# Graph-convolution passes: the load of a block's keys moved ahead of a store, and an index copy moved ahead of ScalarE's one-hots

## The reference

```python
def gcn_conv(x, w, b, row, col, ew, n):
    h = x @ w
    deg = jax.ops.segment_sum(ew, col, num_segments=n)
    dinv = jnp.where(deg > 0, jax.lax.rsqrt(deg), 0.0)
    norm = dinv[row] * ew * dinv[col]
    out = jax.ops.segment_sum(norm[:, None] * h[row], col, num_segments=n)
    return out + b
```

## Time and profile before

| | |
|---|---|
| median of 3 runs | 13451.6 us (13446.46 to 13469.0) |
| the profiled execution, its time | 13464.2 us |
| the profiled execution, its span | 13462.3 us |
| DVE busy over the span | 10894.3 us (81%) |
| PE busy over the span | 9747.7 us (72%) |
| POOL busy over the span | 8948.1 us (66%) |
| ACT busy over the span | 5666.9 us (42%) |

### The profile page before, as it was taken

One profiled execution on the slowest core, in us unless ns is written; L12 is line 12 of the kernel. 1 busy time (PEld: TensorE's weight loads), 2 busy tenths in 40 slices (PEclk: granted clock), 3 DMA queues, 4 the chain that ended last, 5 costly groups with the idle time before them and its releaser, 6 DMA issues. The chain is left out here.

```text
span 13462.3 us, 216102 instructions
## 1 busy us (share of the span) xinstructions
PE 9747.7 (72%) x59425; PEld 8272.6 (61%) x59425; DVE 10894.3 (81%) x23907; ACT 5666.9 (42%) x15747; POOL 8948.1 (66%) x9054
## 2 busy tenths in 40 slices
PE   5666667777756767766764556996997899678886
PEld 4555556666645555555553115886886899667775
DVE  8888878887858888888887996775776888689997
ACT  3444434444423333333333333664564455223332
POOL 6777757776667777777776004666666777677776
PEclk8888879999968888888886666998998999789997
DMA  3333323433323333333334772221221222133332
GB/s 90 89 86 88 89 71 119 124 119 116 121 60 101 101 97 99 100 101 101 100 97 164 272 272 57 49 50 40 49 49 41 54 55 56 32 78 87 85 87 68
DMA packets 627763, 1250.19 MB, mean 93 GB/s; under 512 B 201329, under 2 KB 380982, under 8 KB 577122
## 3 DMA queue, kind: packets, MB, share of 16 engines
q1 hardware_dynamic: 322624, 922.04, 19.8%
q0 software_dynamic: 290752, 265.79, 11.1%
q10 hardware_dynamic: 14337, 61.82, 1.2%
HBM read 482.46 MB, written 768.08 MB: 93 GB/s over the span
## 5 line engine op out<-in xcount | busy, mean ns | idle before, releaser
L1049 PE MATMUL p_slots<-part,one_lo 128*128 128x208 f32 (+1 forms) x20384 | 2841.9, 302 | 360.1 <-ACT one_lo L1016 304.5
L1049 PEld LDWEIGHTS p_slots<-part,one_lo 128*128 128x128 f32 x20384 | 2779.2, 197 | 423.0 <-ACT one_lo L1016 330.2
L995 POOL DMA_INDIRECT rows<-gcn_table,index x2156 | 2132.2, 989 | 1104.5 <-issue 591.3
L1376 PE MATMUL a_p_slots<-att_part,a_one_lo 128*128 128x456 f32 x8232 | 2008.4, 409 | 587.0 <-DVE y L1439 504.4
L1376 PEld LDWEIGHTS a_p_slots<-att_part,a_one_lo 128*128 128x128 f32 x8232 | 1742.2, 214 | 957.1 <-DVE y L1439 684.4
L1307 POOL DMA_INDIRECT sent<-a_out_rows,a_place x1568 | 1584.0, 1010 | 494.9 <-issue 475.6
L623 PE MATMUL p_slots<-x_part,key_lo 128*128 128x448 f32 x6916 | 1676.5, 398 | 114.8 <-DVE scratch L752 78.4
L557 POOL DMA_INDIRECT msg<-x_rows,index x1372 | 1309.3, 954 | 509.1 <-issue 448.1
L557 POOL DMA_INDIRECT msg<-h_rows,index x1274 | 1230.6, 966 | 529.0 <-issue 384.9
L623 PEld LDWEIGHTS p_slots<-x_part,key_lo 128*128 128x128 f32 x6916 | 1399.9, 209 | 234.4 <-DVE scratch L752 95.5
L789 DVE SCALAR_TENSOR_TENSOR run<-run,keep,msg 128x129 f32<-128x129 f32 (+1 forms) x3136 | 1116.7, 356 | 399.9 <-ACT msg L592 295.4
(11 more groups left out here) (481 smaller groups left out, 18358.1 us busy)
## 6 DMA issues: line engine op xcount, KB each, us to landing
running_dst<-a_run SPq DMA_DIRECT2D x98, 1600.0 KB
running_src<-s_run SPq DMA_DIRECT2D x98, 1600.0 KB
running<-run SPq DMA_DIRECT2D x98, 1032.0 KB
running<-run SPq DMA_DIRECT2D x98, 1024.0 KB
running<-y SPq DMA_DIRECT2D x98, 656.0 KB
s_rows<-sent ACTq DMA_DIRECT2D x98, 584.0 KB, 6.9
begun_x<-zeros SPq DMA_DIRECT2D x98, 512.0 KB
a_xdst<-begun_x SPq DMA_DIRECT2D x98, 512.0 KB
```

The source lines that it names most:

```text
L995: pool.indirect_dma_start(out=rows[h][:, KS[h] + k, :], out_offset=None, in_=table, in_offset=offsets(index[h][:, k:k + 1])).then_inc(gath ...
L1049: ins = nc.tensor.matmul(to, one_lo[h][:, q, e:e + P], flat(part[:, q, :, :]), start=q == 0 and part_no == 0, stop=q == CLASSES - 1 and pa ...
L1376: ins = nc.tensor.matmul(to[:, k, 0:WIDE_COLUMNS], one_lo[h][:, q, e:e + P], part[:, q, :], start=q == 0 and part_no == 0, stop=q == WIDE_ ...
```

## The change

In SP's order, the load for block n + 1's parity (it brings the keys of block n + 3) now stands ahead of the store of block n; the first load and the last two stores stand outside the loop. In ACT's order, `stage_index` stands ahead of `light`. Nothing else changes: the same instructions with the same waits are there.

```diff
@@ graph_pass, sync engine @@
-            with sp.Fori(0, IT) as i:
+            def renew(h, n):
+
+                sp.wait_ge(stepped, INIT + per * (n - 1) + ONE_HOTS)
+                sp.sem_inc(sig["rounds"].sem, 1)
+                sp.wait_ge(lit.sem, lit.base + n + 1)
+                load(h, n + 2)
+
+            def store(h, n):
+
+                sp.wait_ge(copied, n + 3)
+                sp.dma_start(running_v[:, bass.ds(n * B, B), :], run_rows[h][:]).then_inc(stored[h], 16)
+
+            renew(0, 0)
+            with sp.Fori(0, IT - 1) as i:
                 for h in range(2):
                     n = 2 * i + h
-
-                    sp.wait_ge(stepped, INIT + per * (n - 1) + ONE_HOTS)
-                    sp.sem_inc(sig["rounds"].sem, 1)
-                    sp.wait_ge(lit.sem, lit.base + n + 1)
-                    load(h, n + 2)
-
-                    sp.wait_ge(copied, n + 3)
-                    sp.dma_start(running_v[:, bass.ds(n * B, B), :], run_rows[h][:]).then_inc(stored[h], 16)
+                    renew(1 - h, n + 1)
+                    store(h, n)
+            renew(1, 2 * IT - 1)
+            for h in range(2):
+                store(h, 2 * IT - 2 + h)
@@ graph_pass, scalar engine @@
+                    act.wait_ge(gathered[h], 16 * GATHERED[h] * (i + 1))
+                    stage_index(h, (n + 2) * B)
+
                     act.wait_ge(looked, 2 * n + 4)
                     light(h, n + 2, i + 2)
-
-                    act.wait_ge(gathered[h], 16 * GATHERED[h] * (i + 1))
-                    stage_index(h, (n + 2) * B)
```

## The result

The changed kernel takes 13133.2 us (median of 4 runs, 13117.58 to 13146.72) against 13455.94 for the kernel before (4 runs): a ratio of 0.9759, 95% interval 0.9742 to 0.9776. The forecast was 13164 with a range down to 13138. The direction and the mechanism were right; the gain is 323 us in place of 288, and the time lies 5 us beyond the range's fast end.

The account below looks back on a forecast made before the run. A circle of waits through ACT's keys was taken to bound passes 1 and 2, POOL to bound pass 3. Savings of 129 + 147 + 14 - 2 = 288 us gave 13164 us, range 13138 to 13240.

Parts of the forecast that it names:

- Everybody waits for ACT, and ACT waits for a DMA behind a store.: Passes 1 and 2: a circle of copy, store, load and light sets the pace; ACT waits 352.9 us for keys.
- ACT's wait for keys goes to nothing; the tightest reserve is DVE's one-hots with 0.75 us.: Passes 1 and 2: keys land 6 us early; one-hots are ready at 7.25 us, PE wants them at 8.0.
- The light's wait for gathers stays within its 2.8 us: Passes 1 and 2: light has 2.8 us to spare; gathers landing later than that after PE's end would delay PE.
- PE's floor 16.9 to 17.47, the clock at 1.00.: Passes 1 and 2: 152 matmuls a pair take 16.9 us in a row, 17.47 without overlap between blocks, at clock 1.00.
- I take 17.1 us a pair: POOL's floor.: Passes 1 and 2: 13 gathers of 1.004 us plus 0.31 us gaps set the pair, saving 129 and 147 us.
- The ends of the passes, 14 us.: Ends of passes 1 and 2: two loads no longer wait for stores, saving 6.9 us in each, 14 together.
- Pass 3: POOL stays the bound, so 0: Pass 3: gathers on POOL keep setting the pair at 23.0 us, so moving the loads gains 0.
- 2 us lost at the end: Pass 3: light behind the gathers is hidden except in the last block, which shows about 2 us more.
- The rest of the kernel keeps its time.: Outside the counted gains: no change, with the spread of runs taken as 5 us below the median and 17 above.
- The strict lock: Rival for passes 1 and 2, chance 0.03: both one-hots block POOL fully, 19.6 us a pair, 13399 us in all.
- POOL held more often: Rival for passes 1 and 2, chance 0.13: busier DVE holds gathers more, 17.4 to 17.7 us a pair, 13221 at 17.7.

Follow-up runs that it names:

- load_only: Changed kernel with ACT's old order (light ahead of row numbers), so only the load moves ahead of the store; ratio 0.9773 to the kernel before.
- index_only: Kernel before with only ACT's order changed: row numbers ahead of light, store still ahead of load; ratio 0.9985 to the kernel before.
- less_pe: Changed kernel with 8 matmuls fewer per block (second table part left out for one looked-up row of each group); pass 1 took 17.18 us a pair.
- control_after: The changed kernel run again, unchanged; 13160.0 us.
- two_inputs: Changed kernel with DVE's two one-hots made by tensor_tensor with a broadcast second input instead of tensor_scalar; pass 1 took 17.90 us a pair.
- pause_longer: Changed kernel with a 320-element DVE memset of a scratch tile between the wait for gathers and the product in pass 3; ratio 0.9763 to the kernel before.

## Why the prediction was wrong by a little

Its steps, in its order:

- *Everybody waits for ACT, and ACT waits for a DMA behind a store.* Right; load_only and index_only show it from both sides.
- *ACT's wait for keys goes to nothing; the tightest reserve is DVE's one-hots with 0.75 us.* Right: PE is never kept waiting in 94 pairs. The light's wait for gathers stays within its 2.8 us.
- *PE's floor 16.9 to 17.47, the clock at 1.00.* Right: 16.98 and 1.00. Of the 2.87 us that a pair of pass 1 won, 1.79 were idle time of PE ((932.80 - 848.48) / 47) and 1.07 were busy time (18.05 busy us become 16.98). Up to 0.49 of that can be that blocks now follow each other without a break (17.47 less 16.98); the rest went with the clock's rise from 0.96 to 1.00.
- ***"I take 17.1 us a pair: POOL's floor."*** The first term that was mis-sized: the pair takes PE's 16.98. The gap of 0.31 us behind the 17.1 was the mean of a row whose longest entry is 1.4 us, so it held some real waits; where POOL has none, the gap is 0.305, and 13 x (1.0027 + 0.3052) is 17.0. Nor is the mean gather a constant: it is 0.992 in load_only, 1.003 here and 1.015 in less_pe. The passes gave 134.9 and 152.5 us, against 129 and 147: 11 us more.
- *The ends of the passes, 14 us.* Right: PE's pause between the last lookup and the next matmul shrank by 7.2 us in pass 1 (14.78 to 7.54), against 6.9.
- ***"Pass 3: POOL stays the bound, so 0"***, and 2 us lost at the end. The second mis-sized term; the 2 us did not show either, since from PE's last lookup to the end of the span both kernels take nearly the same, 1882.2 and 1882.8. POOL is still the bound, but its floor moved: 42 pairs took 957.00 us in place of 966.00, 9 less. 18 long gathers in place of 36 in the last 35 pairs, each 0.5 us longer than the median, would be (36 - 18) x 0.49 / 35 = 0.25 us a pair, about the 0.21 (9 / 42) that it lost. Which blocks meet a long one is decided within a few hundredths of a us, by where a gather's start falls against a product's start; the same program had 36 and 32, and 18 and 26. Why the changed order of loads leads to fewer stays open.
- *The rest of the kernel keeps its time.* True of the program, but the first two profiled executions were 25 us apart ahead of pass 1, and the range took the spread of runs as 5 us below the median only. This third term was too small: the changed kernel's executions lie between 13117.58 and, with the one of control_after, 13160.0, which lies inside the range.

Put together: 134.9 + 152.5 + 14 + 9 = 310 us in the passes against 288, near the 312 and 316 us by which the two programs differ from pass 1 to the end. The other 323 - 312 = 11 us, between medians and traces, are located by no run; ahead of pass 1 executions of one program differ by more than that (8267.8 and 8297.9). With the 310 the sum would have come to 13452 - 310 = 13142, still inside the range: the last step past the range's end is left to the spread, taken as 5 us, and the side on which the four runs fell was chance as far as the traces tell. The range's fast end also took 16.9 for the pair but 0 as the best case for pass 3, and that bound was not one.

The strict lock (0.03) did not come; "POOL held more often" (0.13) did not either in the changed kernel, with a mean of 1.0027 against 1.004, but less_pe showed it in a weaker form than its 17.4 to 17.7: 144 gathers in place of 96 are long in pass 1 and the pair takes 17.18.

## What to carry to other kernels

In a queue that is worked in order, put what a consumer waits for ahead of what has to wait for that same consumer: a load behind a store that waited for ACT made ACT wait for its own output, and 3 us of DMA landing entered every step. When a wait is removed, work out the floor of every engine over the whole step before taking the gain, and use rows where that engine has no wait (a mean gap holds waits too). An engine at its floor in another stage still has a floor that depends on who works beside it, so "0 there" needs a bound on both sides.

## What the runs showed of the hardware

- A DVE operation can hold a gather in two ways. A gather that is under way can have its end pushed to 0.12 us behind the operation's end: with one-hots by tensor_scalar 94 of 96 long gathers of the changed kernel's pass 1. Or a gather that begins while the operation runs ends 0.80 to 0.83 us behind its end: with tensor_scalar 67 of 144 long ones in less_pe; with a tensor_tensor whose two inputs are in SBUF all 186 in two_inputs, and all 161 that began 0.045 us or more behind the product's start in pass 3. The first way was not seen with such a tensor_tensor. The Trainium skill, SBUF — State Buffer, section "Who interferes with whom", says that both kinds can contend with GpSimd, the first through a port pair taken as a lock, the second only with an instruction that reads SBUF. The traces agree that both hold gathers (long in 96 of 609 and 104 of 610), and the second way fits a gather that has to read its row numbers first; that it reads them then is argued, no run shows it.
- A memset of 320 fp32 elements per partition in SBUF, with the product right behind it, held all 20 gathers that began 0.050 us or more behind its start (pause_longer). A memset without an operation behind it was not tried.
- The hold costs at most 0.7 us per event in pass 1 of the changed kernel and depends on phase, that is, on where in DVE's step a gather begins: with work taken from PE the mean gather rose from 1.003 to 1.015 us, which made a kernel with less work slower, 17.18 us a pair against 16.98.
- Short idle times of PE, at most 2.5 us, went with a granted clock of 0.95 and 0.96 over passes 1 and 2 of the kernel before; without them it was 1.00. Not all idle time went with a lower clock: in pass 1 of less_pe PE was idle for 69.1 us, at most 1.8 at a time, and the clock was 1.00.
